# V products of two head groups in one bank, one transposing matmul for a group's maxima, W1 and W2 in one buffer, another order of the first attention, and dummy matmuls

## What is computed

```python
x = L0_attn_x                                     # (8, 512, 128) float32
x = x + attention(layernorm(x))                   # 16 heads of 8, causal, softmax(q k / sqrt(8)) v
x = x + experts(layernorm(x))
# experts(x), x flat as (t, 128):
probs = sigmoid(x @ Wg + bg); weights = probs * (probs > 0.5)
h = relu(einsum('td,edh->eth', x, W1) + b1[:, None, :])
expert_out = einsum('eth,ehd->etd', h, W2) + b2[:, None, :]
combined = einsum('te,etd->td', weights, expert_out)
```

## Time and profile before

| | |
|---|---|
| three runs | 725.62, 723.68, 724.90 us; median 724.9 |
| profiled execution, its own time | 725.9 us |
| span in the profile | 724.2 us |
| TensorE busy | 674.6 us (93%) |
| VectorE, ScalarE, GpSimd busy | 462.4, 453.2, 371.5 us |
| mean granted TensorE clock | 0.966 of 2.4 GHz |
| chain that ended last | PE 81%, DVE 9%, issue 4%, POOL 3% |

### The profile page before, as it was taken

How to read it: one execution, slowest core, us unless ns; L and a number is a source line. 1 busy time by engine, 2 the same in 40 slices (tenths; PEclk the granted TensorE clock), 3 DMA queues, 4 the chain that set the end, 5 groups by cost and what they waited for, 6 DMA issues and landing times.

```text
span 724.2 us, 13238 instructions
## 1 busy us (share of the span) xinstructions
PE 674.6 (93%) x4515; PEld 456.9 (63%) x4515; DVE 462.4 (64%) x933; ACT 453.2 (63%) x841; POOL 371.5 (51%) x441
## 2 busy tenths in 40 slices
PE   3858787999999999999999999999999999999995
PEld 2423354666766676667666776667666766678774
DVE  7983657766865588656865686667766576435332
ACT  2453555766766776666766686667767666666552
POOL 5261123445645575555555566456455545556564
PEclk9966889999999999999999999999999999999998
DMA  6701113212121103221221113110221101001110
GB/s 185 206 14 36 25 25 83 66 41 54 39 83 55 53 16 92 67 52 32 70 68 54 39 37 100 54 54 2 69 68 53 39 32 46 31 30 46 58 30 14
DMA packets 28673, 40.23 MB, mean 56 GB/s; under 512 B 3936, under 2 KB 12648, under 8 KB 28608
## 3 DMA queue, kind: packets, MB, share of 16 engines
q1 hardware_dynamic: 28080, 39.20, 19.4%
q10 hardware_dynamic: 528, 0.20, 0.1%
HBM read 23.52 MB, written 2.23 MB: 36 GB/s over the span
## 4 chain that ended last, share of the span: by engine, by line
PE 81%; DVE 9%; issue 4%; POOL 3%; SPq 1%; ACT 1%; DMA 0%; POOLq 0%; DVEq 0%; ACTq 0%
PE ring L1163 10%; PE y_bank L1207 9%; PE ring L1090 9%; PE ring L1031 8%; PE ring L1033 8%; PE ring L1032 8%; PE y_bank L1211 8%; PE y_bank L1209 8%; PE ring L1102 5%; PE ring L1037 4%; PE ring L1152 2%; DVE xn L841 2%; DVE pm L944 2%; DVE negmax L944 1%; PE y_bank L1163 1%
## 5 line engine op out<-in xcount | busy, mean ns | idle before, releaser
L695 POOL TENSOR_TENSOR h_lo<-h_all,h_hi 128x512 fp32r<-128x512 f32 x128 | 164.6, 1286 | 153.2 <-ACT h_all L803 148.4
L797 ACT ACTIVATE h_hi<-ring 128x512 fp32r<-128x512 f32 x256 | 153.6, 600 | 114.9 <-PE ring L1033 83.9
L764 ACT ACTIVATE pt<-ring 128x512 f32<-128x512 f32 x315 | 176.1, 600 | 33.3 <-PE ring L1090 31.4
L944 DVE TENSOR_REDUCE negmax<-ring 128x1 f32<-128x512 f32 (+1 forms) x189 | 123.6, 683 | 62.7 <-PE ring L1102 62.0
L688 POOL TENSOR_SCALAR_AFFINE_SELECT pt<-pt 128x512 f32<-128x512 f32 x128 | 79.8, 637 | 115.3 <-ACT pt L764 115.2
L994 DVE SCALAR_TENSOR_TENSOR h_lo<-ring,h_hi 128x512 fp32r<-128x512 f32 x128 | 87.7, 685 | 59.7 <-ACT h_hi L797 59.6
L1207 PE MATMUL y_bank<-h_hi,w_lo 128*128 128x512 f32 x256 | 112.5, 440 | 3.5 <-DVE f_buf L1007 1.7
L1031 PE MATMUL ring<-x2T_lo,w_hi 128*128 128x512 f32 x256 | 108.3, 423 | 0.0
L1090 PE MATMUL ring<-stack 32*128 32x512 f32 (+3 forms) x1005 | 93.6, 371 | 13.2 <-DMA stack<-nmT 2.6
L1033 PE MATMUL ring<-x2T_hi,w_hi 128*128 128x512 f32 x256 | 101.1, 395 | 0.0
L1032 PE MATMUL ring<-x2T_hi,w_lo 128*128 128x512 f32 x256 | 101.1, 395 | 0.0
...
## 6 DMA issues: line engine op xcount, KB each, us to landing
...
pt<-in_L_ffn_W SPq DMA_DIRECT2D x1, 2048.0 KB, 10.0
...
```

Of the source, the lines that this page charges most:

```text
L695: g_.tensor_tensor(h_lo[:, (i * SLOTS + s) % 3, :], h_all[:], h_hi[:, (i * SLOTS + s) % 3, :].bitcast(F32), ALU.subtract).then_inc(s_hlo_p ...
L764: sc.activation(pt[:, slot, :], b[:], ACT.Exp, scale=SCALE).then_inc(free_sem("ex", i, g, u), 1)
L797: sc.activation(h_hi[:, (i * SLOTS + s) % 3, :], bank_of("z", i, s)[:], ACT.Relu).then_inc(s_hhi, 1)
L944: v.tensor_reduce(dst, src, AX.X, ALU.max, negate=True).then_inc(free_sem("max", i, g, u), 1)
```

## The change

The V products of an even group and of the odd group after it go into the same bank: VectorE writes V of an odd group's heads 9 columns further to the right, the even group starts the accumulation and the odd one continues it, so that one copy (`og`), one set of four transposes (`oT`) and one division, twice as wide, serve two groups. The maxima of a group are laid out in one 128x128 tile, so one matmul transposes them; they then go to `stack` in two DMAs instead of one. W1 is loaded into `f_buf`, where W2 comes later; the W2 load waits for the last W1 product, and the exponentials no longer wait for W1. Four slots of 32 (7, 15, 23, 31) move from GpSimd's splits to VectorE's. The planner gets other costs, other `SWITCH_DUE` and `PV_DUE`, a table of shifts of due times (`SHIFT`, by engine, kind, and whether it is sequence 0), and a lag of 18 units for `ex` in the first visits. While the ring still has its eighth bank and TensorE has nothing ready in the plan, it writes `warm` into the order: a matmul of 256 bf16 columns whose result nobody reads. There are 131 of them.

```diff
-POOL_SPLITS = [s for s in range(SLOTS) if s % 2 == 1]
+POOL_SPLITS = [s for s in range(SLOTS) if s % 2 == 1 and s % 8 != 7]
...
 EXP_LAG = 12
-FFN_LAG = 55
+HEAD_LAG, HEAD_UNITS = 18, 50
+FFN_LAG = 54
...
 ENTER = {"full": 190, "mask": 92, "scores": 190, "pv": 98}
-SWITCH_DUE = 0.3
-PV_DUE = 0.3
+SWITCH_DUE = 1.5
+PV_DUE = 2
 AFTER_PE, AFTER_OTHERS, AFTER_DMA = 175, 85, 2000
 
+OVERLAP = {"act": 100, "dve": 85, "pool": 40}
...
+SHIFT = {('act', 'exp', False): 2,
+         ('act', 'hhi', False): 3.5,
+         ('act', 'nm', True): -5.5,
+         ('dve', 'hlo', False): -7.0,
...
+         ('pe', 'nm', False): -35.5,
+         ('pe', 'oT', False): -1.5,
+         ('pe', 'xT', False): 3,
+         ('pe', 'y', False): 1,
+         ('pe', 'y', True): 0.5,
...
+         ('sp', 'mrow', False): -11}
...
-    return [([("max", *n) for n in units[k:k + 2]],
-             [("ex", *n) for n in units[max(k - EXP_LAG, 0):max(k - EXP_LAG + 2, 0)]])
-            for k in range(0, len(units) + EXP_LAG, 2)]
+    result, done = [], 0
+    for k in range(0, len(units) + EXP_LAG, 2):
+        lag = HEAD_LAG if k <= HEAD_UNITS else EXP_LAG
+        while done < k - lag:
+            result.append(([], [("ex", *n) for n in units[done:done + 2]]))
+            done += 2
+        ex = units[done:done + 2] if done <= k - lag else []
+        done += len(ex)
+        result.append(([("max", *n) for n in units[k:k + 2]], [("ex", *n) for n in ex]))
+    return result
...
-            before.append((engine, latest[(engine, item[0])]))
+            before.append(("turn", (engine, latest[(engine, item[0])])))
...
+        due += SHIFT.get((engine, item[0], item[1] == 0), 0)
...
-    put("sp", ("w2load", None), -8.9, 600, ("sp", ("stack", 0, 0)))
+    put("sp", ("w2load", None), -8.9, 600, ("pe", ("w1", EXPERTS - 1)))
...
-    put("dve", ("b1", None), -13.9, 2500, ("dma", ("small", None)), ("dve", ("xT", 0)))
-    put("dve", ("vset", None), -10, 1200, ("dve", ("klo", 0)))
+    put("dve", ("b1", None), -13.9, 4200, ("dma", ("small", None)), ("dve", ("klo", 0)))
+    put("dve", ("vset", None), -10, 1800, ("dve", ("klo", 0)))
...
-        put("pe", ("w1", e), -13 + e, 1300, ("dma", ("w1", None)), ("pool", ("center", None)),
+        put("pe", ("w1", e), 10 + 2 * e, 1300, ("dma", ("w1", None)), ("pool", ("center", None)),
...
-        put("act", ("w2", e), 5 + e, 600, ("dma", ("w2", None)))
-        put("pool", ("w2", e), 5 + e, 1280, ("act", ("w2", e)))
...
+        put("act", ("w2", e), 24 + e, 600, ("dma", ("w2", None)))
+        put("pool", ("w2", e), 24 + e, 1280, ("act", ("w2", e)))
...
-                put("dve", ("smax", i, g, u), at + .4, 690, ("pe", ("max", i, g, u)))
+                put("dve", ("smax", i, g, u), at + .4, 690, ("pe", ("max", i, g, u)),
+                    *[("dve", ("merge", *ago[1]))] * (u == 4))
...
-                put("act", ("exp", i, g, u), at + .3, 600, ("pe", ("ex", i, g, u)),
-                    ("pe", ("w1", EXPERTS - 1)))
-            put("dve", ("merge", i, g), t0 + 8 * g + 6.1, 330,
+                put("act", ("exp", i, g, u), at + .3, 600, ("pe", ("ex", i, g, u)))
...
+            if g % 2:
+                put("act", ("og", i, g), at + .6, 600, ("pe", ("pv", i, g)), ("pe", ("oT", i - 1, g)))
+                put("pe", ("oT", i, g), at + 1, 450, ("act", ("og", i, g)))
+                put("dve", ("oT", i, g), at + 1.1, 860, ("pe", ("oT", i, g)), ("pe", ("OT", i - 1)))
+        put("pe", ("OT", i), at + 1.5, 450, ("dve", ("oT", i, 1)), ("dve", ("oT", i, 3)))
...
-        return "act", ("og", *item[1:])
+        return "act", ("og", item[1], item[2] | 1)
...
     def fill(item):
+        if item[0] == "pv" and item[2] % 2:
+            use[item] = use[(*item[:2], item[2] - 1)]
+            return
...
-        at(now + cost, "idle", engine)
+        at(now + cost - OVERLAP.get(engine, 0), "idle", engine)
+        at(now + cost - OVERLAP.get(engine, 0), "turn", key)
...
+        elif banks == EARLY_RING and free and masks_made:
+
+            bank = min((n for n in range(banks) if holder[n] is None), key=lambda n: emptied_at[n])
+            order["pe"].append(("warm", bank, turns[bank]))
+            form = "full"
+            idle["pe"] = False
+            at(now + UNIT_COST // 2, "idle", "pe")
...
-        nm = sb("nm", [P, TB, P], F32R)
-        nmT = sb("nmT", [8, 2, T], F32R)
+        nm = sb("nm", [P, P], F32R)
+        nmT = sb("nmT", [8 * TB, 2, P], F32R)
...
-        rden = sb("rden", [P, TB, GH])
+        rden = sb("rden", [P, TB, GH, 2])
...
-        w1_in, w2_in = pt[:, PT_SLOTS - EXPERTS:, :], f_buf
+        w1_in = w2_in = f_buf
...
                 elif kind == "w2load":
+                    sp.wait_ge(*full("w1", EXPERTS - 1))
...
-                    sp.dma_start(rows[M_ROW::M_STEP, :, 0, :],
-                                 nmT[:, g % 2, :].bitcast(F32)).then_inc(s_mrow[g], 16)
+                    for n in range(2):
+                        sp.dma_start(rows[M_ROW::M_STEP, n, 0, :],
+                                     nmT[16 * n:16 * n + 16, g % 2, :].bitcast(F32)
+                                     ).then_inc(s_mrow[g], 16)
...
-                        act.wait_ge(s_mrow[n % GROUPS], 16 * (n // GROUPS + 1))
-                    sc.activation(nmT[:, g % 2, :], b[0:8, :],
+                        act.wait_ge(s_mrow[n % GROUPS], 2 * 16 * (n // GROUPS + 1))
+                    sc.activation(nmT[:, g % 2, :], b[0:8 * TB, 0:P],
                                   ACT.Copy).then_inc(free_sem("nm", i, g), 1)
...
                     if u == 0 and n >= 2:
-                        act.wait_ge(*full("pv", *divmod(n - 2, GROUPS)))
+                        act.wait_ge(*multiplied(n - 2))
                     elif u == 4 and n >= 1:
-                        act.wait_ge(*full("pv", *divmod(n - 1, GROUPS)))
+                        act.wait_ge(*multiplied(n - 1))
...
-                    sc.activation(o_grp[:, g % 2, :], bank_of("pv", i, g)[:],
+                    if i:
+                        act.wait_ge(*full("oT", i - 1, g))
+                    sc.activation(o_grp[:, g // 2, :], bank_of("pv", i, g)[:],
                                   ACT.Copy).then_inc(free_sem("pv", i, g), 1)
...
-                    v.memset(v_sb[:, :, :, HD:HD + 1], 1.0).then_inc(s_vset, 1)
+                    for o in range(2):
+                        v.memset(v_of[:, :, o, :, (HD + 1) * o + HD:(HD + 1) * (o + 1)],
+                                 1.0).then_inc(s_vset, 1)
...
-                    v.tensor_tensor(v_sb[:, :, :, 0:HD],
-                                    b[:].rearrange("p (t h d) -> p t h d", t=TB, d=HD),
-                                    bv[:].rearrange("p (a h d) -> p a h d", a=1, d=HD)
-                                    .broadcast_to([P, TB, HEADS, HD]),
-                                    ALU.add).then_inc(free_sem("v", i), 1)
+                    src = b[:].rearrange("p (n o j d) -> p n o j d", o=2, j=GH, d=HD)
+                    bias = bv[:].rearrange("p t (a o j d) -> p (t a) o j d", o=2, j=GH, d=HD)
+                    for o in range(2):
+                        last = v.tensor_tensor(v_of[:, :, o, :, (HD + 1) * o:(HD + 1) * o + HD],
+                                               src[:, :, o], bias[:, :, o], ALU.add)
+                    last.then_inc(free_sem("v", i), 1)
...
+                    if u == 4:
+                        wait(dve, s_merge, 2 * (i * GROUPS + g))
...
-                    o = b[:].rearrange("p (t h d) -> p t h d", t=TB, h=GH)
-                    if i and g == 0:
+                    o = b[:].rearrange("p (t j d) -> p t j d", t=TB, j=GH)
+                    if i and g == 1:
                         dve.wait_ge(*full("OT", i - 1))
-                    v.reciprocal(rden[:], o[:, :, :, HD]).then_inc(s_rden, 1)
-                    dve.wait_ge(s_rden, i * GROUPS + g + 1)
-                    v.tensor_tensor(o_tok[:, :, g * GH * HD:(g + 1) * GH * HD]
-                                    .rearrange("p t (h d) -> p t h d", h=GH),
-                                    o[:, :, :, 0:HD],
-                                    rden[:].rearrange("p t (h a) -> p t h a", a=1)
-                                    .broadcast_to([P, TB, GH, HD]),
-                                    ALU.mult).then_inc(free_sem("oT", i, g), 1)
+                    v.reciprocal(rden[:], o[:, :, :, HD:2 * HD + 2:HD + 1]).then_inc(s_rden, 1)
+                    dve.wait_ge(s_rden, 2 * i + g // 2 + 1)
+                    for k in range(2):
+                        n = (g - 1 + k) * GH * HD
+                        last = v.tensor_tensor(o_tok[:, :, n:n + GH * HD]
+                                               .rearrange("p t (j d) -> p t j d", j=GH),
+                                               o[:, :, :, (HD + 1) * k:(HD + 1) * k + HD],
+                                               rden[:, :, :, k:k + 1].broadcast_to([P, TB, GH, HD]),
+                                               ALU.mult)
```

(25 more changed lines are left out.)

100 lines of the change are left out of this document (59 added, 41 removed).

## The result

The changed kernel takes **685.75 us** (median of four runs, 684.83 to 686.44) against 724.86 us for the kernel before (median of four, 723.68 to 725.62, three of them those shown above); the ratio is 0.946, interval 0.944 to 0.948, 39.1 us less. Predicted were 677 us, range 667 to 690, of which the main case had 671 to 682; the result lies in the whole range, outside of the main case's. The profiled execution took 686.2 us, its span is 684.4.

A forecast was written before the change was run, and what follows sets the result against it. Prediction: V products in series with VectorE's maxima set the head's cost, TensorE bounds the rest; 90 us to z0 plus 586.6 behind it is 676.6, 677 from the median; 8 in 10 between 667 and 690.

The forecast's parts named there:

- main case: Whole kernel: 677 us, own range 671 to 682, with z0 from 84 to 95; chance 0.66.
- z0: End of the head: start of the feed-forward part's first W1 product; 118.4 us before, predicted 90, bounds 85 and 97.
- rival (a): Head stays longer, each slip of the order being behind dummies: z0 95 to 110, 682 to 697 us; chance 0.12.
- the 3.3 us of that step: Head, VectorE: normalising x took 4.44 us beside W2 splits on GpSimd; without a split beside it, 3.3 us less.
- 131 dummy matmuls ... 15.7 us: Head, TensorE's list at full rate: dummies at 0.12 us each; 66 us in all with them, 50 without.
- Rival (c): Head: the full clock comes only for half of it; z0 at 116, 703 us; chance 0.05.
- Rival (d): Head: the clock never comes and dummies are pure load; z0 at 142, 729 us, slower; chance 0.03.
- these signs: Head profile: clock above 0.9 between 30 and 90 us, V products below 3 us, VectorE's transpose waits near 5, not 25.
- The o_grp term: Behind z0: 14 sets of o_grp transposes instead of 27, at 0.45 us each, save 5.9 us.
- The nm term: Behind z0: one matmul instead of four transposes nm, 0.36 us saved for each of 26 groups, 9.4 us.
- One cost that I had put at nothing: Behind z0: four more splits per sequence on VectorE (4 x 0.68 us), taken as hidden; without cover 2.7 us a sequence.
- Rival (e): Behind z0: TensorE isn't at its limit, so cutting its list gives nothing; 692.6 us, 693 by the median; chance 0.05.

The follow-up runs named there:

- the early dummies: Changed kernel plus 38 dummy matmuls right behind the small products for the gates and b2, where TensorE stands idle for the first stack: 683.05 us, ratio 0.941.
- the experiment: Changed kernel with the four transposes of o_grp issued twice for each of the 16 pairs: 692.62 us, ratio 0.955.
- The old order: The change's structure without dummies, ordered by the numbers of before (lags 12 and 55, due times 0.3, empty shift table), against the kernel before: 705.58 us, ratio 0.972.

## Why the prediction was right, and where it was off

The mechanisms were right in kind, but not the size of the head, and the range held with some luck. z0 at 100.5 us is above both upper bounds that I gave it, 95 and 97. The time is within 667 to 690 since half of rival (a) was put into that range, and the miss is smaller since 2.7 us came back behind z0.

**z0.** The failed term is "I take 5 us of waits: z0 at 90". The other terms of that sum came out: VectorE's first maximum at 24.2 us (24.0), its work 60.3 us (60.9), and W2's splits, which I had over at 65, end at 69.5, far from z0. The normalisation of x beside which no split stands takes 1.10 us for four in place of 4.44, so the 3.3 us of that step, and the Trainium skill's rule on the shared port ("SBUF — State Buffer", section "SBUF: two separate sides"), agree with the trace. The 24.2 us is two errors that cancel: the splits of b1 took 2.9 us instead of 4.4, so VectorE was free at 23.1; then it waited 1.0 us for the first scores, as the stack, which I had as there, let TensorE start at 23.12 only. The waits from there on are some 16 us. By experiment and trace they are of three kinds:
- about 2.8 us come from TensorE at half rate until about 31 us. I had the clock from the V products on, and did not look at what the moved W1 products leave behind: an idle 4.8 us ahead of the first visit, without dummies. Shown, by the early dummies.
- 8.5 us stand right behind V products of 2.36 us. "A V product has visits ahead of it whose maxima VectorE can work on" was true of one of five. What would have told it: a visit is two maxima, 1.3 us of VectorE's work, so 2.3 us of V product with what hangs on it want two visits of lead in the ring. That V products come through to z0 is shown in one profiled execution, and its size is open; of the last of these waits, up to 1.36 us is a mask that came late.
- the rest, some 5 us, I put down to banks that ScalarE's exponentials empty too late; this was read from the waits and not tested.

**Rival (a)** comes nearest in numbers (z0 95 to 110, 682 to 697 us), but its mechanism fell: "each slip is behind dummies" would have given several us back when half of them went, and it was at most 0.7 to 0.9.

**The dummies' price.** "131 dummy matmuls ... 15.7 us" on a list that is "just full with them": they do fill TensorE (74.6 of 76.5 us), but leaving out half of them gave 0.9 us at most, since they run where it has nothing else. What all of them cost as load can't be measured, as with fewer the clock goes. "50 without" was wrong: it is 50 us at full rate, and without dummies the clock isn't full. My step "the dummies fill gaps as such, so I take the clock to be mostly granted" was right and is worth 9.3 us, more than I saw, as I never priced the order without them. Rival (c), a clock that comes for a part of the head, is where the kernels with a quarter of the dummies and with none go (with none the head's mean clock is 0.82, z0 at 110.3). Rival (d), a clock that never comes with dummies running, fell.

**The clock** is 1.00 in each stretch of 3 us that I looked at from 33 us on, V products take 2.36 us, and the transposes' waits are gone: these signs came as told.

**Behind z0** 586.6 was predicted and 583.9 came. The o_grp term (5.9) is exact in the experiment (6.0). The nm term (9.4) arrives as 6.0 when put back. The tail gave 3.5 us from the last output but one to the last, where I had 3.2; the wait for GpSimd (1.18) is gone. Two following outputs come 1.9 us closer, not 2.3. So the gain behind z0 is 2.7 us more than my terms, and 5.7 more if nm's is taken as 6.0 (21.9 - 6.0 - 6.0 - 3.5 - 1.4 + 0.7). The old order has 586.7 us there, with the gate's product (0.7) ahead of z0, so about 3.5 of them come with the new order; the rest stays open. One cost that I had put at nothing is not nothing: with more work on VectorE, TensorE's waits for xn went from 0.4 to 5.5 us and take a part of nm's saving back (its idle time as a whole grew by 3.0 us, within the 4 that I allowed above). The old order with the new structure has 1.7 us of them and 2.8 us for `xT_lo`, the step behind, so about as much comes with the structure; whether it is the four more splits per sequence was not tested. **Rival (e)** fell: TensorE is at its limit there but for these waits, as its start-to-start times said, against the rule of the Trainium skill ("Perfetto Trace Analysis", section "Identifying the Most-Contended Engine"), by which 353.6 of 519.5 us of weight loading (68%) would leave it headroom.

**The parts of the 39 us**, each the difference of two medians: the structure 20 (725.6 to 705.6), in the profiled executions all behind z0 (the splits that move to VectorE and W1's new place were not tried by themselves); the order 10.5 (to 695.1); the dummies 9.3 (to 685.8). 38 early dummies would give 2.7 more. With half of the later ones left out as well it is 682.31 us, interval of the ratio 0.939 to 0.942, the lowest median of a full version, but not clear of the 683.05 with all of them.
